# Last pass of a four-layer graph network on Trainium2: ScalarE, not SyncE, issues the reads of the stored target one-hots

## The chip, the cores and the metric

The kernel runs on one core of a Trainium2 chip. The metric is the device time of one launch in microseconds (us); lower is better. The engines of the core run their own instruction streams side by side: TensorE (PE; its weight loads are PEld), VectorE (DVE), ScalarE (ACT), GpSimd (POOL) and SyncE (SP), which here only issues transfers. An engine's sequencer (PEq, ACTq, SPq and so on) handles register steps, semaphore waits and DMA issues. Sixteen DMA engines carry every transfer, whichever engine issued it; SP's transfers stand in queue q1 of the profile, ScalarE's in q10, GpSimd's in q0.

## The reference

A graph of 12,500 nodes with 212,500 edges goes through four pre-norm layers with 32 features; the edges are sorted by target. The change touches only the last layer:

```python
def _L3_gnn_ref(x, src, dst):
    n = x.shape[0]
    msg_sum = jax.ops.segment_sum(x[src], dst, num_segments=n)
    deg = jax.ops.segment_sum(jnp.ones_like(dst, dtype=x.dtype), dst, num_segments=n)
    return msg_sum / jnp.maximum(deg, 1.0)[:, None]
...
h = jnp.maximum(_layernorm(x, axis=-1), 0.0)
x = x + _L3_gnn_ref(h, src, dst)
return x
```

Each node receives the mean of the normalised rows of the nodes that point at it.

## The kernel before

Three of the layers' passes sum rows over edges by matmuls against one-hots, pass `s == 1`, `s == 2` and `s == 4`. The last, `s == 4` (`h == 2` in the code), is the one that changes. Part of the edges, in **blocks** of 32 columns of 128 edges, is sorted by source into 49 buckets of 256 nodes. A block is worked in eight **batches** `q` (`BATCHES`): batch 0 has seven buckets, the others six. For a batch, four engines work one behind another:

- SP spreads the edges' low source numbers over the partitions (`spread_low`, L691, writes `lows`, which the profile calls `idx_a`). It may do so once VectorE has compared the batch four before (`s_from`).
- VectorE compares them with the partition numbers, which gives the source one-hots (`compare_sources`, L1892).
- TensorE picks the source rows with them (`pick`, L1308), and ScalarE copies the picked rows out of PSUM into one of four buffers (`pick_block`, L1004; the profile calls the buffers of `q % 4` = 0, 1, 2, 3 `mem_a`, `mem_b`, `more_rows`, `more_rows`).
- TensorE adds them to the target window with the target one-hots (`send`, L1325) and raises `s_sent`. TensorE's order is pick of batch m+1, send of m, pick of m+2, send of m+1, and so on.

The **target one-hots** of a batch lie in one of four buffers in `O` (`to_oh[4]`, `TO_RING[4]` = 4). They are made in one of two ways. Blocks that the first pass had already seen were stored in `targets_d` then; in the last pass these are read back (`return_targets`, L709). The others are compared again on VectorE (`compare_targets`, L1902). Three blocks make one **turn** (`UNIT[4]` = 3), 24 batches, and there are 13 turns. In blocks e = 0 and e = 1 of a turn the batches 0, 1, 2, 4, 5 and 6 are read back, and batches 3 and 7 are compared (`COMPARED`). In block e = 2 all are compared. That is 156 reads in the pass. The three blocks sum into `ps_t`, `ps_z` and `ps_h`, so these names tell e = 0, 1, 2 in the profile. A read for batch m+2 writes the buffer that the send of m-2 read, so it may be issued once that send is done:

```python
sp.wait_ge(s_sent, ((BEFORE[h] + e) * NBATCH + q + 3 - TO_RING[s]) + i * (UNIT[s] * NBATCH))
```

SP issues at step m first the low numbers of batch m+4, then the one-hots of batch m+2, each behind its own wait and in one queue. Beside this, irregular groups are gathered by GpSimd (L793; ScalarE lays out its row numbers, L907) and summed by TensorE (L1194), four groups a turn.

Of the kernel before, what the change touches and what calls it, by code (L numbers as in the profile page):

```python
# [24 lines left out]
P = 128  # L25
# [22 lines left out]
W2 = 256  # L48
# [4 lines left out]
BATCHES = [(0, 7)] + [(7 + 6 * q, 6) for q in range(7)]  # L53
NBATCH = len(BATCHES)
# [6 lines left out]
TO_RING = {1: 2, 2: 2, 4: 4}  # L61
# [56 lines left out]
def gnn_kernel(nc, x, src, dst, et16, et86, ew, ew1, w0, comp0, w1, b1, w2, comp2, selfw,  # L118
# [14 lines left out]
    with ctx:  # L133
# [357 lines left out]
        def carry_wait(eng):  # L491


            eng.sem_inc(s_carry, 1)
# [63 lines left out]
        def block_of(s, n):  # L558

            turn, e = divmod(n, UNIT[s])  # L560
            return e * TURNS[s] + turn

        def turn_group(s, i, f, k):

            return gathered(s, i, k) + f * (gathered(s, 1, k) - gathered(s, 0, k))
# [25 lines left out]
        def _(sp):  # L591
# [100 lines left out]
                             lows_d[bass.ds(i * (NBK * CAP) + (block_of(s, e) * NBK + b0) * CAP, n * CAP)].partition_broadcast(P)  # L692
                             ).then_inc(s_bc[q % RING], 16)

            def kept_rows(i, n, q):

                b0 = BATCHES[q][0]
                return targets_d[bass.ds(i * P + n * P, P), b0 * W2:(b0 + BATCHES[q][1]) * W2]

            def keep_targets(i, f, q):  # L700

                sp.wait_ge(s_made, (f * NBATCH + q + 1) + i * NBATCH)
# [27 lines left out]
            def spread_and_return(h, ahead, soon, returned):  # L730

                s = (1, 2, 4)[h]
                n = UNIT[s] * NBATCH

                def spread(i, f, m):
                    spread_low(h, i, (f + m // n) * UNIT[s] + m % n // NBATCH, m % NBATCH)

                def give_back(i, f, m):
                    if m % n // NBATCH in returned and (s == 2 or m % NBATCH not in COMPARED):
                        return_targets(h, i, (f + m // n) * UNIT[s] + m % n // NBATCH, m % NBATCH)  # L740

                def turn(i, f, last):
                    for m in range(n):
                        if m + ahead < n or not last:
                            spread(i, f, m + ahead)
                        if m + soon < n or not last:
                            give_back(i, f, m + soon)

                for m in range(ahead):
                    spread(0, 0, m)  # L750
                for m in range(soon):
                    give_back(0, 0, m)
                with sp.Fori(0, TURNS[s] - 1) as i:
                    turn(i, 0, False)
                turn(0, TURNS[s] - 1, True)
# [9 lines left out]
            sp.wait_ge(s_from, BEFORE[2] * NBATCH + RING)  # L765
            edge_array(idx_a, et86, s_et86)
            store_nodes(3, 3, lambda i: cols(H, i, D))
            spread_and_return(2, 4, 2, RETURNED)

            for i in range(NB):  # L770
                sp.wait_ge(blk[4]["u_ready"], i + 1)
# [78 lines left out]
        def _(act):  # L850
# [100 lines left out]
            def pick_and_lay_out(s, h):  # L951
# [43 lines left out]
                            if q % 4 == 2 and (q >= 6 or not first) and q < NBATCH + 4:  # L995
                                next_pair(act, i * TURN + (f + q // NBATCH) * TURN, made, stage_pair)

                def pick_block(i, e):
                    for q, (b0, n) in enumerate(BATCHES):
                        b, at = q % 2, ((BEFORE[h] + e) * NBATCH + q) + i * (UNIT[s] * NBATCH)  # L1000
                        act.wait_ge(s_got, at + 3)
                        act.wait_ge(s_sent, at - 1)
                        carry_wait(act)
                        nc.scalar.copy(slot_rows[q % 4][:, 0:n, :], picked_rows(b)[:, 0:n, 0:SPLIT]).then_inc(s_slot, 1)  # L1004
                        if q in HIDDEN4[e]:
                            lay_out_next(s, i, HIDDEN4[e][q])

                if s == 4:
                    with act.Fori(0, TURNS[s]) as i:
                        for e in range(UNIT[s]):  # L1010
                            pick_block(i, e)
                else:
                    pick_weighed(0, 0, True, False)
                    with act.Fori(0, TURNS[s] - 2) as i:
                        pick_weighed(i, 1, False, False)
                    pick_weighed(0, TURNS[s] - 1, False, True)
# [1462 lines left out]
```

## Time and profile before

| | |
|---|---|
| median of 3 runs | 7553.54 us (7550.62 to 7555.81) |
| the profiled execution | 7557.19 us, its span 7555.4 us |
| last pass, picks to sends | 6901 to 7508 us of the span |
| busy over the whole span | PE 64%, PEld 54%, DVE 59%, ACT 32%, POOL 69% |

Times in the rows are microseconds from the start of the span. A row of the timeline has start, duration, engine, line, operation, output<-input, shapes and count; in brackets stands how long the engine was idle before it and what ended that. In the rows of the chain a DMA piece has its start (the issue), its time to landing, and its tensors. In the rows by stretch (windows) stand the length of the stretch, then for PE, PEld, DVE, ACT and POOL the busy time with the number of instructions, then TensorE's granted clock (1.00 is the full 2.4 GHz), the mean busy share of the 16 DMA engines, and GB/s.

### The profile page before, as it was taken

The numbers are of one execution on the slowest core, as the hardware profiler recorded it, in microseconds if no ns is written. First come the engines' busy times: TensorE is split into PE (matmuls) and PEld (weight loads), VectorE is DVE, ScalarE is ACT, GpSimd is POOL, SyncE is SP. The second block draws the span as 40 slices with busy tenths as digits, with TensorE's granted clock in tenths as the row PEclk, the third lists the DMA queues.
The fourth block names the chain that finished last, engine by engine and source line by source line (L and its number), as shares of the span: only waits on it lengthen the run. The fifth ranks groups of instructions, "written<-read, shape, count | busy, mean of one in ns | idle before, by whom it ended". The sixth has DMA issues, their size and how long they took to land. (4 is left out here: it accounts for less than half of the span.)

```text
span 7555.4 us, 149897 instructions
## 1 busy us (share of the span) xinstructions
PE 4797.7 (64%) x41375; PEld 4089.9 (54%) x41376; DVE 4473.8 (59%) x13819; ACT 2380.2 (32%) x7420; POOL 5213.8 (69%) x5417
## 2 busy tenths in 40 slices
PE   5333333333335677777777776777777777777888
PEld 2222222222224555556666665677777777776777
DVE  5555555557778888885555554444444444446876
ACT  4444444440002222222555555211111111113332
POOL 2777777777765777774766663677777777775774
PEclk6555555555556666666887887555555555557998
DMA  7000000000003444444898988222222222224775
GB/s 175 14 14 14 14 14 14 14 14 13 13 12 98 128 127 126 127 127 118 288 304 293 307 291 271 60 41 41 41 41 41 41 41 41 41 41 123 218 216 167
DMA packets 547178, 778.01 MB, mean 103 GB/s; under 512 B 226905, under 2 KB 383097, under 8 KB 546997
## 3 DMA queue, kind: packets, MB, share of 16 engines
q1 hardware_dynamic: 317381, 416.33, 18.1%
q0 software_dynamic: 173168, 146.14, 11.8%
q10 hardware_dynamic: 56448, 213.62, 7.2%
q8 instruction: 53, 0.87, 0.0%
q14 instruction: 128, 1.05, 0.0%
HBM read 445.42 MB, written 330.21 MB: 103 GB/s over the span
## 5 line engine op out<-in xcount | busy, mean ns | idle before, releaser
L793 POOL DMA_INDIRECT arena<-table,ibuf x3328 | 3151.2, 947 | 1237.4 <-issue 1123.1
L793 POOL DMA_INDIRECT arena<-nodes,ibuf x2080 | 2059.9, 990 | 967.6 <-issue 635.0
L1194 PE MATMUL ps_agg<-mem_a,arena 128*32 128x80 f32 (+1 forms) x3744 | 472.7, 308 | 566.7 <-DVEq L1647 511.8
L1194 PE MATMUL ps_agg<-mem_b,arena 128*32 128x80 f32 (+1 forms) x3744 | 457.4, 301 | 505.7 <-DVEq L1647 492.2
L1194 PEld LDWEIGHTS ps_agg<-mem_a,arena 128*32 128x32 f32 (+1 forms) x3744 | 414.9, 156 | 626.4 <-DVEq L1647 529.7
L1194 PEld LDWEIGHTS ps_agg<-mem_b,arena 128*32 128x32 f32 (+1 forms) x3744 | 400.5, 152 | 555.6 <-DVEq L1647 515.4
L1463 PE MATMUL ps_agg<-tbuf,msg 128*64 128x80 f32 x2496 | 373.6, 344 | 330.7 <-DVE msg L2140 330.7
L1065 ACT ACTIVATE att<-score 128x8 f32<-128x8 f32 x208 | 43.3, 208 | 1649.0 <-DVE score L2131 1649.0
L1463 PEld LDWEIGHTS ps_agg<-tbuf,msg 128*64 128x64 f32 x2496 | 336.0, 226 | 351.8 <-DVE msg L2140 351.8
L916 ACT ACTIVATE tbuf<-O,tbuf 128x49 bf16<-128x49 bf16 x1664 | 448.5, 363 | 76.7 <-DVE H L1814 76.7
L1892 DVE TENSOR_SCALAR tbuf<-idx_a,pcol 128x768 bf16<-128x768 bf16 (+1 forms) x1040 | 402.7, 429 | 93.8 <-issue 44.9
L1666 DVE TENSOR_TENSOR big<-big,ps_agg 32x80 f32 (+1 forms) x468 | 108.4, 232 | 541.9 <-PE ps_agg L1194 476.6
L2123 DVE TENSOR_TENSOR msg<-arena,ps_z 128x256 f32<-128x256 f32 x208 | 87.7, 422 | 551.6 <-DMA arena<-table,ibuf 551.6
L1640 DVE TENSOR_TENSOR arena<-arena,ew_s 128x256 f32<-128x256 f32 x416 | 177.0, 425 | 360.0 <-DMA arena<-table,ibuf 295.7
L1458 PE MATMUL ps_wide<-yw,mem_b 80*128 80x33 f32 x1680 | 380.6, 403 | 1.2 <-ACT yw L1047 1.2
L1458 PE MATMUL ps_h<-yw,mem_b 80*128 80x33 f32 x1664 | 377.0, 403 | 0.0
L1458 PEld LDWEIGHTS ps_wide<-yw,mem_b 80*128 80x128 f32 x1680 | 366.3, 331 | 19.1 <-issue 17.8
L1458 PEld LDWEIGHTS ps_h<-yw,mem_b 80*128 80x128 f32 x1664 | 362.8, 331 | 17.8 <-issue 17.8
L907 ACT COPY ibuf<-idx_a 128x8 int32 x208 | 39.7, 196 | 933.0 <-DMA arena<-table,ibuf 930.9
L1216 PE MATMUL ps_wide<-O,not_before 128*128 128x392 bf16 x156 | 82.3, 528 | 358.3 <-DVE H L1814 358.3
L1450 PE MATMUL ps_wide<-ident,tbuf 128*80 128x128 f32 x1248 | 297.7, 421 | 0.0
L2174 DVE TENSOR_TENSOR big<-big,ps_agg 64x80 f32 x208 | 47.8, 230 | 401.3 <-PE ps_agg L1463 401.3
(417 smaller groups left out, 11941.6 us busy)
## 6 DMA issues: line engine op xcount, KB each, us to landing
table<-tbuf ACTq DMA_DIRECT2D x294, 544.5 KB
idx_a<-lows_d SPq DMA_DIRECT2D x637, 192.0 KB
targets_d<-tbuf SPq DMA_DIRECT2D x182, 384.0 KB, 2.4
H<-targets_d SPq DMA_DIRECT2D x182, 384.0 KB
arena<-table,ibuf POOLq DMA_INDIRECT x3328, 2.4
O<-targets_d SPq DMA_DIRECT2D x130, 384.0 KB
table<-tbuf ACTq DMA_DIRECT2D x98, 495.0 KB
arena<-nodes,ibuf POOLq DMA_INDIRECT x2080
```

The source lines that it names most:

```text
L793: nc.gpsimd.indirect_dma_start(out=INTO[s][:, k, c, 0:WIDTH[s]], out_offset=None, in_=TABLE[s], in_offset=bass.IndirectOffsetOnAxis(ap=ibu ...
L916: op = nc.scalar.mul(moved[:, j, 2 + part, :], by_bucket[:, j, :], of)
L1194: last = nc.tensor.matmul(ps_agg[ROW0[s]:ROW0[s] + CHN[s], 0:WIN], narrow[:, k, c, 0:CHN[s]], onehots[b][:, c, :], start=(c == 0), stop=(c ...
L1216: nc.tensor.matmul(ps_wide[:, r, 0:392], not_before[:, :], bucket_oh[:, at], start=True, stop=False)
L1450: nc.tensor.transpose(ps_wide[0:WIN, c // 4, (c % 4) * P:(c % 4 + 1) * P], rows[:, c, :], ident[:, :])
L1458: last = nc.tensor.matmul(y_own[b][:, c, :], onehot_t[:, c, :], yw[:, :], start=True, stop=True)
L1463: last = nc.tensor.matmul(ps_agg[0:2 * D, 0:WIN], msg[:, c, :], onehots3[k][:, c, :], start=(c == 0), stop=(c == CH - 1))
L1640: V.tensor_tensor(rows, rows, by[:, of].unsqueeze(2).to_broadcast([P, CH, D]), ALU.mult)
L1666: V.tensor_tensor(into, into, ps_agg[r0:r1, 0:WIN], ALU.add)
L1892: op = V.tensor_scalar(from_oh[s][q % 2][:, a, 0:n * CAP], lows[q % RING][:, 0:n * CAP], pcol2[:, a:a + 1], None, ALU.is_equal)
L2123: V.tensor_tensor(msg[:, :, D:2 * D], gbuf[:, k, :, PAIR:PAIR + D], last_in_ps.unsqueeze(2).to_broadcast([P, CH, D]), ALU.mult)
L2174: V.tensor_tensor(into, into, ps_agg[0:2 * D, 0:WIN], ALU.add)
```

## The change

The reads of the stored target one-hots in the last pass leave SP's stream. SP's call becomes `spread_and_return(2, 4, 0, ())`, so it issues the low numbers alone. ScalarE now issues each read (`ask_targets`, called by `ask_ahead`) directly behind its copy of batch m, for batch m+2, with the same wait on `s_sent`. The first two are issued ahead of the loop. The last turn of ScalarE's loop is written out behind it.

```diff
+                def ask_targets(i, e, q):
+
+                    act.wait_ge(s_sent, ((BEFORE[h] + e) * NBATCH + q + 3 - TO_RING[s]) + i * (UNIT[s] * NBATCH))
+                    carry_wait(act)
+                    act.dma_start(to_oh[s][q % TO_RING[s]][:, 0:BATCHES[q][1], :].rearrange("p k w -> p (k w)"),
+                                  kept_rows(i, block_of(s, e), q)).then_inc(s_there[q % TO_RING[s]], 16)
+
+                def ask_ahead(i, m, last):
+                    e, q = divmod(m, NBATCH)
+                    if (e < TURNS[s] * UNIT[s] or not last) and e % UNIT[s] in RETURNED and q not in COMPARED:
+                        ask_targets(i, e, q)
+
...
                         nc.scalar.copy(slot_rows[q % 4][:, 0:n, :], picked_rows(b)[:, 0:n, 0:SPLIT]).then_inc(s_slot, 1)
-                        if q in HIDDEN4[e]:
-                            lay_out_next(s, i, HIDDEN4[e][q])
+                        ask_ahead(i, e * NBATCH + q + 2, last)
+                        if q in HIDDEN4[e % UNIT[s]]:
+                            lay_out_next(s, i, HIDDEN4[e % UNIT[s]][q], e // UNIT[s])
...
-            spread_and_return(2, 4, 2, RETURNED)
+            spread_and_return(2, 4, 0, ())
...
-                    with act.Fori(0, TURNS[s]) as i:
+                    for m in range(2):
+                        ask_ahead(0, m, False)
+                    with act.Fori(0, TURNS[s] - 1) as i:
                         for e in range(UNIT[s]):
-                            pick_block(i, e)
+                            pick_block(i, e, False)
+                    for e in range(UNIT[s]):
+                        pick_block(0, (TURNS[s] - 1) * UNIT[s] + e, True)
```

ScalarE's stream of the last pass, in block e = 0 of a turn, batches 0 to 2, before (the casts are the copies of picked rows, `ibuf` the row numbers for a gather; the names in brackets are the semaphores waited for):

```order
L1004 CAST mem_a<-ps_wide 128x672 [waits slots_rows_summed]
L1001 REGISTER_ALU
L1002 REGISTER_ALU [waits slots_rows_picked]
L1004 CAST mem_b<-ps_wide 128x576 [waits slots_rows_summed]
L1001 REGISTER_ALU
L1002 REGISTER_ALU [waits slots_rows_picked]
L1004 CAST more_rows<-ps_wide 128x576 [waits slots_rows_summed]
L905 ISA
L907 ISA [waits sum1_gathered_0]
L907 COPY ibuf<-src_i 128x8
```

The same place of the same stream in the changed kernel:

```order
L1016 CAST mem_a<-ps_wide 128x672 [waits slots_rows_summed]
L1000 REGISTER_ALU
L1002 ISA [waits slots_rows_summed]
L1002 DMA O<-targets_d 128x1536
L1013 REGISTER_ALU
L1014 REGISTER_ALU [waits slots_rows_picked]
L1016 CAST mem_b<-ps_wide 128x576 [waits slots_rows_summed]
L1013 REGISTER_ALU
L1016 CAST more_rows<-ps_wide 128x576 [waits slots_rows_picked,slots_rows_summed]
L1002 ISA [waits slots_rows_summed]
L1002 DMA O<-targets_d 128x1536
```

A read with its wait now stands between two copies, except behind the copy of batch 1 (batch 3 is compared), and it stands ahead of the row numbers' wait for a gather. SP's stream in the same pass before, where reads and low numbers take turns:

```order
L690 REGISTER_ALU
L691 ISA [waits sources_compared]
L691 DMA idx_a<-lows_d 128x768
L709 ISA [waits slots_rows_summed]
L709 DMA O<-targets_d 128x1536
L690 REGISTER_ALU
L691 ISA [waits sources_compared]
L691 DMA idx_a<-lows_d 128x768
L709 ISA [waits slots_rows_summed]
L709 DMA O<-targets_d 128x1536
```

And SP's stream there in the changed kernel:

```order
L695 REGISTER_ALU
L696 ISA [waits sources_compared]
L696 DMA idx_a<-lows_d 128x768
L695 REGISTER_ALU
L696 ISA [waits sources_compared]
L696 DMA idx_a<-lows_d 128x768
L695 REGISTER_ALU
L696 ISA [waits sources_compared]
L696 DMA idx_a<-lows_d 128x768
```

The reads with their waits are gone from it, and the low numbers follow one another.

## Rows read from the trace of the kernel before

**Rows 1.** Stretches: the last pass; block e = 0 of its fourth turn.

```profile
6901.00:7508.00 607.00, 489.51 (x6555) 428.05 (x6553) 483.02 (x1748) 207.28 (x364) 423.79 (x404) 0.99 0.72 216
7046.00:7061.00 15.00, 12.99 (x183) 11.73 (x181) 11.48 (x35) 6.02 (x11) 11.65 (x12) 1.00 0.95 296
```

**Rows 2.** Chain of work that ended last, in the last pass: shares, and DMA pieces.

```profile
by line: DMA O<-targets_d 25.4%; DVE O L1902 15.8%; DVE tbuf L1892 12.6%; issue 10.5%; PE ps_agg L1194 7.3%; PE ps_wide L1308 4.7%; PE ps_z L1325 4.2%; PE ps_t L1325 3.9%; DMA idx_a<-lows_d 2.3%; PE ps_h L1325 1.4%; SPq L691 1.3%; DVE mem_a
...
7054.85 5.35 DMA O<-targets_d
7066.32 4.48 DMA O<-targets_d
...
7235.87 6.41 DMA O<-targets_d
...
7468.62 7.59 DMA O<-targets_d
```

**Rows 3.** Waits in the last pass: total us, times, longest.

```profile
DVE tbuf L1892 <- DMA idx_a<-lows_d: 16.2, 24, 1.5
PE ps_z L1325 <- DMA O<-targets_d: 14.4, 26, 1.5
...
PE ps_t L1325 <- DMA O<-targets_d: 8.5, 19, 1.8
```

**Rows 4.** Waits of SP's sequencer in the last pass, same columns.

```profile
SPq L691 <- DVE tbuf L1892: 306.0, 251, 3.5
SPq L709 <- PE ps_t L1325: 15.6, 43, 1.6
SPq L709 <- PE ps_z L1325: 8.1, 13, 0.9
```

**Rows 5.** Timeline of ACT: five copies of the fourth turn, one of the eighth.

```profile
7045.00 0.72 ACT L1004 CAST mem_a<-ps_wide 128x672 bf16<-128x672 f32 x1 [1.42 <-PE ps_wide L1308]
...
7052.17 0.64 ACT L1004 CAST mem_a<-ps_wide 128x576 bf16<-128x576 f32 x1 [2.20 <-PE ps_wide L1308]
...
7055.32 0.64 ACT L1004 CAST more_rows<-ps_wide 128x576 bf16<-128x576 f32 x1 [0.53 <-PE ps_wide L1308]
...
7064.95 0.64 ACT L1004 CAST more_rows<-ps_wide 128x576 bf16<-128x576 f32 x1 [1.06 <-PE ps_wide L1308]
...
7066.52 0.64 ACT L1004 CAST mem_a<-ps_wide 128x576 bf16<-128x576 f32 x1 [0.93 <-PE ps_wide L1308]
...
7237.46 0.64 ACT L1004 CAST mem_a<-ps_wide 128x576 bf16<-128x576 f32 x1 [2.24 <-PE ps_wide L1308]
```

**Rows 6.** Timeline of PE: sends, six of them of batches read back.

```profile
7049.34 0.85 PE L1325 MATMUL ps_t<-O,more_rows 128*96 128x256 bf16 x6 [0.20 <-issue]
...
7053.85 0.82 PE L1325 MATMUL ps_t<-O,mem_a 128*96 128x256 bf16 x6
...
7056.50 0.83 PE L1325 MATMUL ps_t<-O,more_rows 128*96 128x256 bf16 x6 [0.15 <-DMA O<-targets_d]
...
7060.34 0.94 PE L1325 MATMUL ps_z<-O,mem_a 128*96 128x256 bf16 x7 [1.02 <-DMA O<-targets_d]
...
7069.31 0.82 PE L1325 MATMUL ps_z<-O,mem_b 128*96 128x256 bf16 x6
...
7070.94 0.83 PE L1325 MATMUL ps_z<-O,more_rows 128*96 128x256 bf16 x6 [0.30 <-DMA O<-targets_d]
...
7242.42 0.83 PE L1325 MATMUL ps_t<-O,more_rows 128*96 128x256 bf16 x6 [0.57 <-DMA O<-targets_d]
```

**Rows 7.** Timeline of ACT: a copy of batch 0, block e = 1.

```profile
7058.06 0.72 ACT L1004 CAST mem_a<-ps_wide 128x672 bf16<-128x672 f32 x1 [0.94 <-PE ps_wide L1308]
```

**Rows 8.** Line L1001 from 7058 to 7059 us: duration ns, first and last start.

```profile
L1001 ACTq ALU_OP  x1: 35/35/35, 7058.2 to 7058.2; - x1
```

**Rows 9.** Line L1124, 4300 to 4320 us: ScalarE's stores of pass 2, columns as above.

```profile
L1124 ACTq DMA_DIRECT2D table<-tbuf x6: 338/343/343, 4303.1 to 4315.6; - x6
```

**Rows 10.** The page's DMA issues: stores of the same one-hots in pass 1.

```profile
targets_d<-tbuf SPq DMA_DIRECT2D x182, 384.0 KB, 2.4
```

More of the change, by code:

```diff
@@ L561, in block_of, with kept_rows @@
             return e * TURNS[s] + turn
+        def kept_rows(i, n, q):
+            b0 = BATCHES[q][0]
+            return targets_d[bass.ds(i * P + n * P, P), b0 * W2:(b0 + BATCHES[q][1]) * W2]
         def turn_group(s, i, f, k):
@@ L693, in spread_low @@
                              ).then_inc(s_bc[q % RING], 16)
-            def kept_rows(i, n, q):
-                b0 = BATCHES[q][0]
-                return targets_d[bass.ds(i * P + n * P, P), b0 * W2:(b0 + BATCHES[q][1]) * W2]
             def keep_targets(i, f, q):
@@ L996, in pick_weighed, with pick_block @@
                                 next_pair(act, i * TURN + (f + q // NBATCH) * TURN, made, stage_pair)
-                def pick_block(i, e):
+                def ask_targets(i, e, q):
[7 more added lines that the diff above has]
+                        ask_targets(i, e, q)
+                def pick_block(i, e, last):
                     for q, (b0, n) in enumerate(BATCHES):
```

## The prediction

> **What bounds the kernel now.** I read first the stretches of the last pass, then its chain of waits, then the waits by engine, and last one turn in order of time. The stretches [rows 1] show a pass of 607 us in which no engine is full: TensorE is busy 490 us, VectorE 483, GpSimd 424, ScalarE 207, at a granted clock of 0.99. Block e = 0 of a turn stands out: there the DMA engines are 95% busy at 296 GB/s. The chain of waits [rows 2] says what ends last. A quarter of it, 25.4% of 607 us or 154 us, is the time from the issue of a one-hot read to its landing; the low numbers' transfers have 2.3%. So in blocks e = 0 and 1 the loop is a ring: send of batch m-2, issue of the read for m+2, landing, send of m+2. Landings on the chain last from 4.48 to 7.59 us here [rows 2]. TensorE itself stood idle for these reads 14.4 + 8.5 = 22.9 us, 45 times [rows 3]. That is all that a faster read can give it directly; VectorE stood 16.2 us, 24 times, for low numbers [rows 3]. In block e = 2 nothing is read back, and VectorE compares every batch.
>
> **When a read is issued.** Before, SP issues the read for m+2 as soon as it has issued the low numbers of m+4 and the send of m-2 is done. 56 of the 156 reads waited for that send, 23.7 us in all [rows 4]; the others only had to come through behind the low numbers, which wait for VectorE (251 waits, 306 us) [rows 4]. How quick SP is when the send was what it waited for: the send at 7053.85 ends 0.82 us later, at 7054.67 [rows 6], and the read is issued at 7054.85 [rows 2], 0.18 us behind.
>
> After, the read for m+2 stands behind ScalarE's copy of batch m, and that copy needs the pick of m, which TensorE begins only after it issued the send of m-2. So the wait on the send never holds ScalarE up, but every read goes out later by about a pick. The question is whether it is later by the copy too. ScalarE's copy of 0.72 us begins at 7058.06 [rows 7], and its sequencer did the next register step at 7058.2 [rows 8], with the copy still running. I take the issue to come 0.25 us behind the start of the copy: SP's 0.18 and one more step for the second wait. If the DMA must wait for the copy's end, it is 0.64 us more [rows 5]. For the read of batch 0 in block e = 1 that gives 7055.32 + 0.25 = 7055.57 against 7054.85 [rows 5, 2]: 0.72 us later.
>
> **What the added DMA costs ScalarE.** Its own stores hold its sequencer 0.34 us each [rows 9]. 156 of them are 53 us over a pass in which it computes 207 of 607 [rows 1]; where copies follow each other quickest their starts lie some 1.2 us apart (0.53 idle and 0.64 busy [rows 5]), and 0.25 + 0.34 = 0.59 us fits behind a start. I cost it at nothing; the cover is ScalarE's idle time. The row numbers for a gather come 0.4 to 0.6 us later four times a turn; GpSimd is busy 424 us of 607 [rows 1] and has that to spare. The first two reads, ahead of the loop, and the written-out last turn cost nothing that I can find; SP's shorter stream saves SP's time only.
>
> **How long a read takes from ScalarE's queue.** No row shows it. The bounds: stores of the same 384 KB landed 2.4 us after the issue [rows 10], though they write where these read; reads from SP took 4.48 us at 7066.32, 5.35 us for the seven buckets at 7054.85, and up to 7.59 us [rows 2]. In its own queue a read no longer stands behind 192 KB of low numbers, which helps; but both draw on DMA engines that are 95% busy [rows 1], and low numbers issued after the read may now pass beside it. I take 4.5 us for 384 KB, at the short end of what SP's reads show, and 5.0 us for the 448 KB of batch 0.
>
> **The sum, on the fourth turn.** A send may start 0.25 + 4.5 + 0.14 = 4.89 us after its copy began, 5.39 us for batch 0. The 0.14 is the step from landing to matmul: 7066.32 + 4.48 = 7070.80, matmul at 7070.94 [rows 2, 6]. "Later" is measured against before, and a delay of one send shifts all copies whose picks come behind it. The rest of the turn's sends have more room than this.
> - Block 0, batch 2: copy 7045.00 + 4.89 = 7049.89, was 7049.34 [rows 5, 6]: 0.55 later.
> - Block 0, batch 6: 7052.17 + 0.55 + 4.89 = 7057.61, was 7056.50: 1.11 later.
> - Block 1, batch 0: its copy's pick came ahead of that send, so 7055.32 + 0.55 + 5.39 = 7061.26, was 7060.34: 0.92 later. The 1.02 us that TensorE had waited there [rows 6] swallows the 1.11.
> - Block 1, batch 5: 7064.95 + 0.92 + 4.89 = 7070.76, was 7069.31: 1.45 later.
> - Block 1, batch 6: 7066.52 + 0.92 + 4.89 = 7072.33, was 7070.94: 1.39 later, where 0.30 of waiting had been.
>
> The turn ends 1.4 us later. Not all turns are like it: in the eighth the read at 7235.87 took 6.41 us and TensorE waited 0.57 us for it; there 7237.46 + 4.89 = 7242.35 against 7242.42 [rows 2, 5, 6], nothing later. I take 1.0 us a turn as the mean of the two sorts, 13 us over 13 turns. Against it stands what low numbers gain from a queue of their own. At most it is VectorE's 16.2 us [rows 3]; with 2.3% of the chain against 25.4% I take 3 us. Sum: +10 us on the profiled execution's 7557.2, so 7567; that execution lay 3.7 us above the median of the runs, so 7564 us as a median, +0.14%.
>
> How this hangs on the landing: 0.1 us more makes the turn 0.3 us longer, since it enters three times (batch 2, then batch 6 or 0, then batch 5), which is 3.9 us over the pass. A landing of 4.2 us gives 7552, 5.0 us gives 7583.
>
> **A rule against the change.** The stretch [rows 1] has the DMA engines at 95% in block 0, so a second queue finds them taken. The Trainium skill, page "DMA: Bandwidth & Descriptors", section "Issuing engines are not separate DMA queues", says that transfers issued by different engines run on the same 16 DMA engines and interleave, and that issuing from several saves only sequencer time. By it the read would land no sooner and the change would only issue later, which is the rival of landings as long as before; no row here shows a read from ScalarE's queue.
>
> **The rivals.** A measurement of this kernel can tell some 0.2%, 15 us, from no change.
> - Forecast, 0.44: landings of 4.2 to 4.8 us; the later issue and the freer queue nearly cancel. 7552 to 7576.
> - Landings of 4.1 us and less, 0.17: standing behind the low numbers was the greater part of the landing. At 3.8 us the sum is 10 - 0.7 x 39 = -17 us: 7537. The floor is 22.9 + 3 us gained, 7528. For it: the low numbers are issued just ahead of each read. Against it: 95% busy.
> - Landings as long as before, 0.20, slower: I put them at 5.0 us, between 4.48 and 5.35 [rows 2], and with the issue 0.7 us later TensorE waits more. 10 + 0.5 x 39 = 29.5 us: 7583. It decides from a landing of about 4.63 us on, where +15 us is reached. For it: 296 GB/s in block 0 [rows 1].
> - ScalarE holds the DMA until its copy has ended, 0.14, slower: 0.64 us in three places of 13 turns is +25 us, 7589. Against it: [rows 8].
> - Anything else, such as the reads delaying a later copy: 0.05.
>
> **How the numbers follow.** The predicted time is the forecast's, 7564 us. Of its 0.44 about 0.31 lie within 15 us of before and 0.13 above. Of the fast landings 0.12 are below 7538.4. The two slower rivals lie nearly wholly above 7568.6. With the rest shared out: faster 0.14, same 0.41, slower 0.45. The range for 8 in 10 runs from 7538, which leaves out about half of the fast landings, to 7592, above both slow rivals' middles.
>
> **What the profile after would show.** Issues of `O<-targets_d` on ScalarE's sequencer, 0.2 to 0.3 us behind the start of a copy if I am right, 0.9 if the copy holds them. Landing pieces on the chain of 4.4 to 4.6 us, with a share still above a quarter. TensorE's wait for these reads, 22.9 us before, at 30 to 45 us. VectorE's 16.2 us of waiting for low numbers mostly gone. The time of the pass, 607 us, at 613 to 620, and nothing moved ahead of it. I am wrong if landings fall below 4 us, if sends wait for copies rather than reads, or if GpSimd's gathers become what is waited for.

## The result, and the profile after

The changed kernel takes 7625.45 us (7618.71 to 7629.61, 4 runs) against 7554.68 us (7550.62 to 7556.03, 4 runs) for the kernel before: a ratio of 1.0092, interval 1.0077 to 1.0107. That is 71 us slower, and 33 us above the top of my range. The profiled execution took 7629.61 us, with a span of 7627.8. From the first copy of the pass to the last it takes 681.8 us instead of 605.1, which is 77 us more. The pass began 6 us sooner in this execution (6895.6 against 6902.1), so nothing was lost ahead of it: the whole loss lies inside.

I went through the same views as before. First the stretches of the changed kernel: the pass, and then three neighbouring pieces of its fourth turn (columns as in [rows 1]).

```profile
6895.00:7580.00 685.00, 516.03 (x6557) 454.25 (x6554) 481.70 (x1749) 209.81 (x364) 434.08 (x403) 0.94 0.66 191
...
7067.00:7072.00 5.00, 5.00 (x78) 4.74 (x74) 4.30 (x14) 2.83 (x5) 3.81 (x4) 1.00 0.91 239
7072.00:7076.00 4.00, 0.51 (x6) 0.50 (x6) 0.55 (x2) 0.64 (x1) 3.08 (x4) 1.00 1.02 362
7076.00:7081.00 5.00, 5.00 (x52) 4.56 (x50) 1.38 (x5) 0.64 (x1) 1.46 (x2) 0.66 0.17 58
```

Two things differ from [rows 1]. The DMA share of the pass has fallen from 0.72 to 0.66, and TensorE's granted clock from 0.99 to 0.94. The pieces show how both come about: TensorE runs full for 5 us, stands for nearly 4 us while the DMA engines are completely taken (1.02, 362 GB/s), and then runs full again but at a granted clock of 0.66 over the 5 us, partly at its lower level of 1.2 GHz, while the DMA engines have next to nothing to do (0.17). Where block e = 0 before had a mean DMA share of 0.95 [rows 1], and between 0.90 and 0.99 in pieces of 3 and 4 us, there are now bursts and gaps.

The waits of the changed kernel in the pass (total us, times, longest), and SP's below them:

```profile
POOL arena L793 <- DVEq L1677: 94.1, 44, 4.5
...
PE ps_z L1342 <- DMA O<-targets_d: 60.7, 26, 3.8
...
DVE tbuf L1909 <- DMA idx_a<-lows_d: 26.3, 22, 3.1
...
PE ps_t L1342 <- DMA O<-targets_d: 21.9, 16, 2.6
```

```profile
SPq L696 <- DVE tbuf L1909: 481.6, 273, 8.1
```

TensorE waits for reads 60.7 + 21.9 = 82.6 us where it was 22.9 [rows 3], and not more often (42 times instead of 45): the waits are longer. They lie nearly all in three places of a turn: block 0 batch 2, block 1 batch 0 and block 1 batch 5, with 1.42, 2.59 and 2.08 us a turn, where it was 0.35, 0.81 and 0.12 us (means of the 13 turns in the trace). VectorE waits 26.3 us for low numbers instead of 16.2 [rows 3]; a queue of their own gave them nothing. SP stands 481.6 us for VectorE's comparison where it stood 306.0 [rows 4], which costs nothing in itself. GpSimd's gathers wait 94.1 us for VectorE, where it was 23.4, but the waits have no line in which an engine waits for a gather.

ScalarE's stream, in order of time, with the issue of a read behind a copy, and two more within 2.6 us:

```profile
7055.45 0.34 ACTq L1002 DMA_DIRECT2D O<-targets_d  x1
...
7068.44 0.64 ACT L1016 CAST more_rows<-ps_wide 128x576 bf16<-128x576 f32 x1 [0.53 <-PE ps_wide L1325]
7068.68 0.34 ACTq L1002 DMA_DIRECT2D O<-targets_d  x1
...
7069.82 0.34 ACTq L1002 DMA_DIRECT2D O<-targets_d  x1
...
7071.23 0.36 ACTq L1002 DMA_DIRECT2D O<-targets_d  x1
```

And SP's low numbers at that time, five issues in 6 us:

```profile
7067.02 6.02 SPq L696 DMA_DIRECT2D idx_a<-lows_d  x5
```

TensorE over the same time. The two waits are for the reads issued at 7055.45 and at 7068.68:

```profile
7061.68 0.85 PE L1342 MATMUL ps_t<-O,more_rows 128*96 128x256 bf16 x6 [2.36 <-DMA O<-targets_d]
7062.46 2.00 PE L1211 MATMUL ps_agg<-mem_a,arena 128*32 128x80 f32 x16
7064.39 1.14 PE L1325 MATMUL ps_wide<-ew_s,tbuf 128*128 128x96 bf16 x12
...
7067.62 0.67 PE L1325 MATMUL ps_wide<-half_tiles,tbuf 128*128 128x96 bf16 x12
...
7075.53 0.94 PE L1342 MATMUL ps_z<-O,mem_a 128*96 128x256 bf16 x7 [3.49 <-DMA O<-targets_d]
7076.40 2.26 PE L1211 MATMUL ps_agg<-mem_b,arena 128*32 128x80 f32 x16
7078.59 1.14 PE L1325 MATMUL ps_wide<-arena,tbuf 128*128 128x96 bf16 x12
```

The same sixteen matmuls of an irregular group took this long in the kernel before, behind the wait of 1.02 us at 7060.34 [rows 6]:

```profile
7061.20 1.29 PE L1194 MATMUL ps_agg<-mem_b,arena 128*32 128x80 f32 x16
```

After the wait of 3.49 us they take 2.26 us instead of 1.29, and the pick behind them 1.14 us for twelve matmuls where 0.67 is usual. A wait like these is paid for a second time. Counted in the trace's clock records, from 5 us behind the first copy to the last, TensorE was at its lower level for 75.1 us, against 3.4 us before. If it had been busy all that time, the same work would have taken 37 us at the full clock, so up to 37 us of the 77 may lie there. Not every long wait has this behind it: of TensorE's 22 waits for reads over 2 us, 14 had a stretch at the lower level that began in them or within 2 us behind them. The others, among them waits of 3.39 and 3.56 us, had none.

The page's queues (packets, MB, share of the 16 engines) and its issues show that the reads moved and that nothing was added. q1 had 416.33 MB before and q10 213.62, so 63 MB went from the one to the other:

```profile
q1 hardware_dynamic: 294917, 353.27, 15.5%
...
q10 hardware_dynamic: 78912, 276.68, 9.7%
...
O<-targets_d ACTq DMA_DIRECT2D x130, 384.0 KB
```

The chain of waits of the changed kernel can't be read over the whole pass, since it has no piece between 6950 and 7450 us. Two landings behind that are these, of 448 and of 384 KB, and both are longer than the 5.0 and 4.5 us that I counted on:

```profile
7540.60 5.48 DMA O<-targets_d
...
7550.85 6.13 DMA O<-targets_d
```

### The profile page after: what moved, and what is told of

It is laid out like the page before. It is cut to its first block and busy times, and to the rows that moved or that the text cites. A ratio compares the mean times of both kernels' runs of the same rounds, so it can differ in the third digit from the quotient of the medians.

```text
span 7627.8 us, 149984 instructions
## 1 busy us (share of the span) xinstructions
PE 4799.7 (63%) x41375; PEld 4096.8 (54%) x41376; DVE 4472.5 (59%) x13819; ACT 2387.3 (31%) x7420; POOL 5229.4 (69%) x5417
```

## The experiments

Two things were changed at once: the queue that a read goes through (**two queues** instead of one), and the moment at which it is issued (**late**, behind pick and copy, instead of **early**, as soon as the send allows). My theory was that both count and that they work on each other; the rivals were that the lateness alone costs the time, that the second queue alone does, and that the clock is only a result of waits and costs nothing itself. Each experiment below was timed beside the kernel before; the table gives medians, the ratio with its interval, and, from the profiled execution, waits in the pass and its length from first to last copy.

| kernel | us | before | ratio | TensorE waits for reads | VectorE for low numbers | first to last copy |
|---|---|---|---|---|---|---|
| before | 7554.68 | | | 22.9 | 16.2 | 605.1 |
| changed | 7625.45 | 7554.68 | 1.0092 (1.0077 to 1.0107) | 82.6 | 26.3 | 681.8 |
| two queues, early | 7571.62 | 7558.07 | 1.0019 (1.0009 to 1.0029) | 31.9 | 35.2 | 624.0 |
| one queue (SP), late | 7579.5 | 7558.07 | 1.0026 (1.0016 to 1.0037) | 42.7 | 21.3 | 620.2 |
| one queue (ScalarE), late | 7591.16 | 7556.43 | 1.0043 (1.0026 to 1.0059) | 46.0 | 26.6 | 636.6 |
| one queue (SP), reads first | 7555.58 | 7558.07 | 0.9998 (0.9988 to 1.0008) | 5.7 | 53.9 | 607.1 |
| changed, with filler matmuls | 7606.21 | 7558.07 | 1.0062 (1.0045 to 1.0079) | 50.4 | 22.4 | 658.9 |
| changed, a quarter of the low numbers' bytes | 7564.08 | 7554.56 | 1.0015 (1.0005 to 1.0025) | 37.8 | 3.7 | 616.1 |

A second table has what the ring of the prediction is made of, at the three places where TensorE's long waits lie (in us, means of 13 turns). The first column is the time from the end of the send that a read waits for to the issue of the read, summed over the three places. The landing is the time from the issue to the last mark of completion in the trace. Some marks are missing there, so the landings are rather too short than too long.

| kernel | send to issue, sum of three | landing, block 0 batch 2 | block 1 batch 0 | block 1 batch 5 | their sum | all 156 reads |
|---|---|---|---|---|---|---|
| before | 1.6 | 4.56 | 5.38 | 4.52 | 14.5 | 5.2 |
| changed | 3.2 | 5.36 | 5.96 | 6.18 | 17.5 | 5.1 |
| two queues, early | 0.7 | 4.67 | 6.09 | 3.98 | 14.7 | 5.1 |
| one queue (SP), late | 2.6 | 4.53 | 4.93 | 5.14 | 14.6 | 4.8 |
| one queue (ScalarE), late | 3.3 | 4.66 | 4.97 | 5.24 | 14.9 | 4.7 |
| one queue (SP), reads first | 0.5 | 3.94 | 5.07 | 3.78 | 12.8 | 4.6 |
| changed, with filler matmuls | 3.4 | 5.34 | 6.11 | 5.92 | 17.4 | 5.1 |
| changed, a quarter of the low numbers' bytes | 3.3 | 4.61 | 4.81 | 4.57 | 14.0 | 4.3 |

The mean of all reads hardly differs between before and changed (5.2 and 5.1 us): some reads with time to spare land sooner (block 0 batch 6 after 3.50 us instead of 5.90), and those that TensorE stands for land later.

**Two queues, early.** ScalarE issues the read ahead of its waits for the pick, so that the send of m-2 holds it, but no longer low numbers ahead of it, as on SP before. Against the changed kernel:

```diff
                     for q in range(NBATCH):
...
+                        ask_ahead(i, e * NBATCH + q + 2, last)
...
                         nc.scalar.copy(slot_rows[q % 4][:, 0:n, :], picked_rows(b)[:, 0:n, 0:SPLIT]).then_inc(s_slot, 1)
-                        ask_ahead(i, e * NBATCH + q + 2, last)
```

> The changed kernel, but ScalarE issues the read for batch m+2 ahead of its wait for the pick of m and its copy, so as early as SyncE did before (send of m-2 done), still from its own queue. Theory A (the lateness of about a pick does it): the pass is back at its old length, 7545 to 7560 us. Theory B (two queues side by side do it: a read of a burst shares the DMA engines with low numbers issued after it, where one queue served it first; and each TensorE wait of over 2 us then halves its clock for some microseconds): the issue comes 0.7 to 1 us earlier, which takes some of the clock drops away, but landings in a burst stay at 6 us and more; 7575 to 7605 us.

It is 14 us slower than before: the second queue alone costs that, although the reads go out a little sooner than on SP (0.7 us against 1.6 over three places). Its waits, in a profiled execution that was the slowest of its ten, 11 us above their median:

```profile
DVE tbuf L1909 <- DMA idx_a<-lows_d: 35.2, 33, 2.9
...
PE ps_z L1342 <- DMA O<-targets_d: 26.6, 23, 3.0
...
PE ps_t L1342 <- DMA O<-targets_d: 5.3, 14, 1.7
```

Neither side gained from being apart. The low numbers are waited for twice as long as before (35.2 against 16.2 [rows 3]), and they took a share of the chain that they had not had:

```profile
by line: DVE O L1919 18.8%; DMA O<-targets_d 17.8%; DVE tbuf L1909 12.1%; issue 10.8%; DMA idx_a<-lows_d 10.2%; PE ps_agg L1211 5.9%; PE ps_wide L1325 5.3%; PE ps_t L1342 4.9%; PE ps_z L1342 3.5%; PE ps_h L1342 1.8%; DVE mem_a L2134 1.6%; D
...
7015.27 7.84 DMA O<-targets_d
...
7058.59 6.25 DMA O<-targets_d
```

The low numbers' 10.2% stand against 2.3% in [rows 2]. My reading is that one queue had served the two streams in the order of their issue, and that with two queues a transfer that is needed next gets only a part of the sixteen engines. The landings at block 1 batch 0 fit that (6.09 us instead of 5.38); at the other two places they are not longer.

**One queue, late.** SP keeps the reads, but waits in the last pass for the pick of batch m instead of for the send of m-2. Against the kernel before:

```diff
-                sp.wait_ge(s_sent, ((BEFORE[h] + e) * NBATCH + q + 3 - TO_RING[s]) + i * (UNIT[s] * NBATCH))
+                if s == 4:
+                    sp.wait_ge(s_got, ((BEFORE[h] + e) * NBATCH + q + 1) + i * (UNIT[s] * NBATCH))
+                else:
+                    sp.wait_ge(s_sent, ((BEFORE[h] + e) * NBATCH + q + 3 - TO_RING[s]) + i * (UNIT[s] * NBATCH))
```

> The kernel before, but SyncE holds the read for batch m+2 until the pick of batch m is done, which is about when ScalarE issues it in the changed kernel (0.15 us earlier); one queue as before. Low numbers behind a held read go out later too. Theory A (lateness): 7600 to 7625 us. Theory B (two queues and the clock): the ring is 0.7 us longer in three places a turn, without the long landings: 7565 to 7585 us.

It is 21 us slower than before. Its waits:

```profile
PE ps_z L1328 <- DMA O<-targets_d: 31.9, 38, 2.4
...
DVE tbuf L1895 <- DMA idx_a<-lows_d: 21.3, 26, 1.7
...
PE ps_t L1328 <- DMA O<-targets_d: 10.8, 19, 1.0
```

So lateness costs 21, the second queue 14, and both together 71. This run is not quite as late as the changed kernel, though: SP issues the read 0.02 us behind the start of the copy, ScalarE 0.23 us (medians), so the send to issue is 2.6 us a turn here and 3.2 there. The next experiment has the full lateness. Neither of the rivals with a single cause holds. TensorE was at its lower clock for 6.8 us here and for 27.3 us in the experiment before, against 75.1 us with both.

**One queue on ScalarE, late.** The low numbers go to ScalarE too, so that one queue carries both again. Against the changed kernel:

```diff
-            spread_and_return(2, 4, 0, ())
...
+                def ask_lows(i, m, last):
+                    e, q = divmod(m, NBATCH)
+                    if e < TURNS[s] * UNIT[s] or not last:
+                        b0, n = BATCHES[q]
+                        act.wait_ge(s_from, ((BEFORE[h] + e) * NBATCH + q + 1) + i * (UNIT[s] * NBATCH))
+                        act.dma_start(lows[q % RING][:, 0:n * CAP],
+                                      lows_d[bass.ds(i * (NBK * CAP) + (block_of(s, e) * NBK + b0) * CAP, n * CAP)].partition_broadcast(P)
+                                      ).then_inc(s_bc[q % RING], 16)
...
+                        ask_lows(i, e * NBATCH + q + 4, last)
...
+                    for m in range(RING):
+                        ask_lows(0, m, False)
```

> Repeat, since in the first try all programs ran some 36% slower. The changed kernel with the low numbers, too, issued by ScalarE, those of batch m+4 ahead of its copy of batch m; the reads stay late, behind the copy. One queue, ScalarE's. Theory B (two queues side by side): 7565 to 7590 us. Rival C (ScalarE's queue or its late issue alone): 7610 to 7630 us or more.

It is 35 us slower than before, with twice as many DMAs issued by ScalarE as in the changed kernel, and yet 36 us less slow than that one. So ScalarE as the issuer isn't what costs 71 us; two queues in place of one is a large part of it.

```profile
PE ps_z L1353 <- DMA O<-targets_d: 33.9, 33, 2.3
...
PE ps_t L1353 <- DMA O<-targets_d: 12.1, 14, 1.7
```

No wait reaches 2.4 us, and TensorE spent 17.1 us at its lower clock. This is the better measure of the lateness alone: 35 us, where the run on SP, with reads issued 0.7 us a turn sooner, has 21. With 14 us for the second queue, 22 us of the 71 are left that neither brings alone (36 us by the run on SP). The second table shows where they lie. Landings at the three places sum to 14.5 us a turn before, to 14.6 and 14.9 with lateness alone, to 14.7 with the second queue alone, and to 17.5 with both. 3.0 us a turn are 39 us over the pass.

**One queue, the read first.** In the kernel before, the two transfers of a step change places: SP issues the read for m+2 ahead of the low numbers for m+4.

```diff
+                        if s == 4 and (m + soon < n or not last):
+                            give_back(i, f, m + soon)
...
-                        if m + soon < n or not last:
+                        if s != 4 and (m + soon < n or not last):
                             give_back(i, f, m + soon)
```

> The kernel before, but at each step of the last pass SyncE issues the read for batch m+2 ahead of the low numbers of m+4, not behind them; one queue. If standing behind 192 KB of low numbers lengthens a read, landings on the chain fall from 4.4 to 5.9 us to about 4 us and the time to 7535 to 7550 us. If the low numbers, held up by a read's wait, become late instead, VectorE's 16.2 us of waiting for them grows: 7555 to 7575 us.

The time doesn't change (0.9998). Its waits:

```profile
DVE tbuf L1894 <- DMA idx_a<-lows_d: 53.9, 53, 2.7
...
PE ps_z L1327 <- DMA O<-targets_d: 3.0, 5, 1.1
...
PE ps_t L1327 <- DMA O<-targets_d: 2.7, 5, 1.0
```

The order in one queue only moves the wait from one stream to the other: 22.9 us for reads became 5.7, 16.2 us for low numbers became 53.9. So in one queue nothing is to be gained by serving the reads first: the low numbers are just as close behind.

**Filler matmuls in the wait.** In the changed kernel TensorE does 18 matmuls whose results nobody reads ahead of the wait for the read of batch 2 of blocks that are the first of a turn, and 34 ahead of batch 0 of the second. These are two of the three places with the long waits; at the third, batch 5 of block 1, 1.74 us a turn are left here.

```diff
+                        for j in range({(0, 2): 18, (1, 0): 34}.get((e % 3, q), 0)):
+                            nc.tensor.matmul(ps_agg[:, 256:256 + SPLIT], ident_h[:, :], ident_h[:, 0:SPLIT], start=True, stop=True)
```

> The changed kernel with matmuls that nobody reads put on TensorE ahead of its wait for the read in two places a turn: 18 (about 1.0 us at full clock) ahead of the send of batch 2, block 0, and 34 (about 1.9 us) ahead of batch 0, block 1. They add 13 x 2.9 = 38 us of TensorE work where it idles now. If the clock that falls to half after the long waits costs a large part of the 70 us, the granted clock of the pass is back near 0.99 and the time falls to 7575 to 7600 us. If the clock is only a by-product, the time stays at 7620 to 7640 us.

TensorE over the same two places of the fourth turn:

```profile
7060.24 0.93 PE L1338 MATMUL ps_agg<-ident_h 128*128 128x96 bf16 x18
7061.44 0.85 PE L1344 MATMUL ps_t<-O,more_rows 128*96 128x256 bf16 x6 [0.27 <-ACT more_rows L1016]
7062.22 1.29 PE L1211 MATMUL ps_agg<-mem_a,arena 128*32 128x80 f32 x16
...
7070.61 1.61 PE L1338 MATMUL ps_agg<-ident_h 128*128 128x96 bf16 x34
7073.69 0.94 PE L1344 MATMUL ps_z<-O,mem_a 128*96 128x256 bf16 x7 [1.47 <-DMA O<-targets_d]
7074.56 1.29 PE L1211 MATMUL ps_agg<-mem_b,arena 128*32 128x80 f32 x16
```

The group of sixteen takes 1.29 us again in both places. The kernel has 13 x (0.93 + 1.61) = 33 us more work for TensorE, and is 19 us faster than the changed one (7606.21 against 7625.45; 23 us when each is set against its own runs of the kernel before). Its waits for reads fell by 32 us, about what the filler fills:

```profile
PE ps_z L1344 <- DMA O<-targets_d: 39.5, 24, 2.8
...
PE ps_t L1344 <- DMA O<-targets_d: 10.9, 13, 1.2
```

TensorE stood or did filler for 50.4 + 33 = 83 us, as long as it stands in the changed kernel without filler (82.6). Nor did reads land much sooner at the three places (17.4 us a turn against 17.5). So the gain isn't from shorter landings, and what else differs is the clock, at the lower level for 13.7 us instead of 75.1. I put its share of the 71 us at about 20 us. What the same filler does to the kernel before could not be measured.

**A quarter of the low numbers' bytes.** In the changed kernel the transfers of low numbers in the last pass, behind the first four, move only the first quarter of each batch. Left out are the other three quarters, where the comparison goes by what the buffer last held; the count of transfers and of all other instructions is the same.

```diff
-                sp.dma_start(lows[q % RING][:, 0:n * CAP],
-                             lows_d[bass.ds(i * (NBK * CAP) + (block_of(s, e) * NBK + b0) * CAP, n * CAP)].partition_broadcast(P)
+                m = n * CAP // (4 if s == 4 and not whole else 1)
+                sp.dma_start(lows[q % RING][:, 0:m],
+                             lows_d[bass.ds(i * (NBK * CAP) + (block_of(s, e) * NBK + b0) * CAP, m)].partition_broadcast(P)
```

> The cut of the low numbers to a quarter in the changed kernel, another try (all programs ran 36% slower in the earlier ones). Theory B (low numbers share the DMA engines with a burst's reads, and that is what makes the read of a burst late): read landings in a burst about 4.5 us, few waits over 2 us, clock of the pass back near 0.99, 7530 to 7570 us. Rival C (late issue or ScalarE's queue in itself): 7590 us and more.

It comes within 9.5 us of the kernel before; 61 of the 71 us are gone.

```profile
PE ps_z L1343 <- DMA O<-targets_d: 28.5, 27, 1.9
...
PE ps_t L1343 <- DMA O<-targets_d: 9.3, 9, 1.2
...
DVE tbuf L1910 <- DMA idx_a<-lows_d: 3.7, 6, 1.2
```

```profile
6915.00:7500.00 585.00, 461.24 (x6212) 404.08 (x6213) 456.47 (x1661) 198.60 (x345) 411.70 (x388) 0.99 0.55 138
```

With less to share, no wait passes 1.9 us and the clock stays at 0.99. The reads go out as late as in the changed kernel (3.3 us a turn), but their landings at the three places are 14.0 us a turn in place of 17.5. So it takes the full traffic of the low numbers to stretch them. The run also has the landings that I had forecast (4.5, 5.0 and 4.5, measured 4.61, 4.81 and 4.57), and took 7564 us, the time of the forecast. That is good for the ring of the prediction, but luck in part: VectorE's waits for low numbers fell by 12.5 us here, where I had counted 3. The same cut might help the kernel before as well, and that control could not be measured. Its waits for both streams sum to 39 us [rows 3]; if it gained all of them, 22 us of the 61 would still be the changed kernel's own. Between 22 and 61 the share stays open, and so does whether it is the order of service or the mere amount of traffic that counts.

**What was not measured.** Twelve further runs, of three controls and of repeats, fell on times in which every program, the kernel before too, took some 36 to 38% longer (10,273 to 10,419 us for the kernel before). No variant differs there by more than 0.22%, not even those that differ above, so they say nothing on the question. They stand here with what was expected of them.

The changed kernel with a quarter of the low numbers' bytes, as above.

> The changed kernel with the low numbers' transfers of the last pass cut to a quarter of their bytes (48 KB in place of 192), after the first four; the rest of the low numbers is left over from earlier batches, so the last layer's sums are left out in this form: the work after the landing is the same. Reads and low numbers still go out from two queues at the same times. Theory B (a read of a burst lands late because the low numbers share the DMA engines with it): the read's landings in a burst fall from 6 to 7 us to about 4.5 us, no TensorE wait is long enough to bring the clock down, and the time lies within 25 us of the same cut made to the kernel before. Rival C (ScalarE's queue is slow in itself, or the ring simply is too long by the late issue): the distance between the two stays at 50 us or more.

Measured: 10281.23 us against 10284.28, ratio 1.0 (0.9983 to 1.0017).

> Repeat of the cut of the low numbers to a quarter in the changed kernel, since the chip ran all programs some 36% slower in the first try. Theory B (low numbers share the DMA engines with a burst's reads): read landings in a burst about 4.5 us, no clock drop from long waits, time within 25 us of the control. Rival C (the late issue or ScalarE's queue in itself): distance to the control 50 us or more.

Measured: 10265.45 us against 10276.86, ratio 1.0001 (0.9978 to 1.0024).

> The cut of the low numbers to a quarter in the changed kernel, third try (all programs ran 36% slower in the first two). By now late reads alone cost some 20 us on SyncE's queue and 35 us on ScalarE's single queue, against 70 us with two queues. Theory B (low numbers share the DMA engines with a burst's reads): read landings in a burst about 4.5 us, no clock drop from long waits, time within 25 us of the control. Rival C: distance to the control 50 us or more.

Measured: 10391.74 us against 10418.74, ratio 0.9986 (0.9965 to 1.0007).

A control: the kernel before with the same cut of the low numbers.

> The control for the one above: the kernel before with the same cut, which leaves out the same part. Both theories: TensorE's 22.9 us of waiting for reads and VectorE's 16.2 us for low numbers fall to a few us; 7525 to 7545 us.

Measured: 10283.45 us against 10284.28, ratio 1.0007 (0.9992 to 1.0022).

> Repeat of the control, the same cut in the kernel before: 7525 to 7545 us by both theories.

Measured: 10250.35 us against 10276.86, ratio 0.9993 (0.9966 to 1.0021).

> The control, the same cut in the kernel before: 7525 to 7545 us by both theories.

Measured: 10428.13 us against 10418.74, ratio 1.0008 (0.9982 to 1.0035).

> The control, another try: the same cut in the kernel before. The changed kernel with the cut took 7564 us. If low numbers in the way of the reads cost the kernel before as well, 7525 to 7545 us, and the late issue alone is worth the 20 to 40 us between the two. If the kernel before is held by something else, 7545 to 7560 us, and with small low numbers the late issue costs next to nothing.

Measured: 10242.41 us against 10272.97, ratio 0.9978 (0.9957 to 0.9999).

> The control, last try: the same cut in the kernel before. The changed kernel with the cut took 7564 us. If low numbers in the way of the reads cost the kernel before as well, 7525 to 7545 us, and the late issue alone is worth the 20 to 40 us between the two. If the kernel before is held by something else, 7545 to 7560 us, and with small low numbers the late issue costs 10 to 20 us.

Measured: 10277.66 us against 10280.28, ratio 0.9997 (0.9974 to 1.002).

One queue on ScalarE, late, as above.

> The changed kernel with the low numbers, too, issued by ScalarE: those of batch m+4 ahead of its copy of batch m, so about as early as SyncE issues them. The reads stay late, behind the copy. All is in one queue again, ScalarE's. Theory B (two queues): like the late reads on SyncE's one queue, 7565 to 7590 us. Rival C (ScalarE's queue or its late issue alone): 7610 to 7630 us, or more, since ScalarE now issues two transfers a batch.

Measured: 10288.55 us against 10284.28, ratio 1.0009 (0.9995 to 1.0023).

A control: one queue on ScalarE, early, both transfers ahead of its waits for the pick.

> The one above, with the reads moved ahead of the copy too: one queue, ScalarE's, and both transfers as early as in the kernel before. If queue number and time of issue are all that matters, 7545 to 7565 us, no difference from before. If issuing from ScalarE costs something in itself (0.34 us of its sequencer for each of two transfers), 7570 us and more.

Measured: 10273.24 us against 10284.28, ratio 0.9993 (0.9973 to 1.0012).

> One queue, ScalarE's, for both transfers, and both as early as in the kernel before. If the number of queues and the time of issue are all that matters: 7545 to 7565 us. If issuing from ScalarE costs something in itself: 7570 us and more, and then 15 us of the distance between the late reads on ScalarE's single queue (7591) and on SyncE's (7579) are explained.

Measured: 10409.88 us against 10418.74, ratio 0.9986 (0.9964 to 1.0008).

A control: the kernel before with the filler matmuls at the same two places.

> Control for the filler: the same matmuls that nobody reads, 2.9 us a turn, in the kernel before, where the waits in these places are 0.2 and 1.0 us and the clock stays up. They should cost 13 x (2.9 - 1.2) = 22 us: 7570 to 7580 us. If they cost less than 10 us, work in these places is free and the filler's gain in the changed kernel is the clock's alone; if the filler gains time here too, it is not the clock that it acts on.

Measured: 10438.45 us against 10418.74, ratio 1.002 (0.9996 to 1.0045).

So it isn't measured how much the filler or the cut would bring to the kernel before.

## Why the prediction was wrong, step by step

**When a read is issued: right.** I gave 0.25 us behind the start of the copy; it is 7068.68 - 7068.44 = 0.24 us (median of the pass 0.23), with the copy of 0.64 us still running. The rival in which ScalarE holds the DMA until its copy has ended is out. ScalarE's 0.34 us for each DMA stayed hidden: TensorE's long waits end with reads, not with copies, and with low numbers on ScalarE as well the kernel was faster than the changed one.

**Which places lengthen: right.** The long waits are at batch 2 of block 0 and batches 0 and 5 of block 1, the three places through which a landing entered my sum. The ring itself holds in size too. Send to issue and landing together are 16.1 us a turn over the three places before, and 1.1 us more with late reads on SP, 2.1 us more with late reads and low numbers on ScalarE, and 4.6 us more in the changed kernel (second table). Times 13 turns that is about 15, 27 and 60 us, where the pass was 15, 32 and 77 us longer. The sends didn't come to wait for copies, and GpSimd's gathers didn't become what is waited for.

**The landing: the term that failed.** I took 4.5 us from issue to landing for 384 KB and 5.0 for 448 KB. The step from issue to matmul, with 0.14 counted in, would have been 4.64 and 5.14. In the fourth turn it was 7061.68 - 7055.45 = 6.23 and 7075.53 - 7068.68 = 6.85 us. Over all 13 turns the landings at the three places were 5.36, 5.96 and 6.18 us (second table), where I had 4.5, 5.0 and 4.5. That is 3.5 us a turn more, and by my own rule 45 us over the pass. I had argued that a read which no longer stands behind low numbers lands sooner. Its first packet does come sooner (384 KB: 1.68 us behind the issue instead of 2.19, medians of 129 reads), but its last doesn't (4.68 instead of 4.57). The rival of landings as long as before was nearer, but no description either: I put it at 5.0 us and 7583 us, and landings stayed as they were only in the mean of all reads. Where TensorE stands for them they grew by 0.6 to 1.7 us. The error below both is that I took one landing for all reads, and took it from reads issued at an even pace. The rule that I set against the change, in the Trainium skill's page "DMA: Bandwidth & Descriptors", section "Issuing engines are not separate DMA queues", held in the direction it gives: issued from two engines, the same transfers landed no sooner on the mean (5.1 against 5.2 us).

**What low numbers gain: wrong in sign.** I counted 3 us gained from a queue of their own. VectorE waits 26.3 us for them instead of 16.2, and 35.2 where the reads are early. In the prediction I wrote that low numbers issued after the read may now pass beside it, and gave that no price.

**What I didn't have at all: the clock, and the bunching.** One is the clock. I priced a wait at its own length. Waits of 2.4 and 3.5 us in the fourth turn are each followed by a stretch at 1.2 GHz, in which the group of sixteen takes 2.0 to 2.3 us instead of 1.29; from the filler I put this at about 20 us. The other is that waits bunch the requests. Behind a long wait several picks and copies follow at once, each asks for a read 1.1 to 1.4 us after the other, and SP adds its own five; so the next reads meet at the DMA engines (1.02) and land late, and then nobody asks (0.17). That landings at the three places are long only with both changes together, and only with the low numbers' full traffic, is measured. That it comes about by this loop of wait and burst is read off the fourth turn and not shown by itself.

The sum with measured values then stands so: 10 us as forecast, 45 us for landings and some 20 us for the clock, which makes 75 for 71 measured. The 3 us that I gave to low numbers as a gain belong on the other side, and how far the terms overlap the runs don't separate; so this is an account of the size and no exact division.

## What to carry to other kernels

Before you give a transfer a queue of its own, ask what it shares the DMA engines with. Here they were 95% busy in block 0, and neither stream gained: reads and low numbers together were waited for 39 us in one queue and 67 us in two. A mean landing hides what matters in a ring of buffers: look up the landing of those reads that an engine stands for, and ask what the next requests do after a wait, since here they came in a burst. When a change lengthens TensorE's waits, read the granted clock behind them too, and price a stretch at the lower level besides the wait itself.

## What the runs showed of the hardware

- Reads of 384 KB had their first packet 2.19 us behind the issue in the kernel before, 1.94 us in a queue of their own with early issue, and 1.91 (SP) and 1.61 us (ScalarE) in one shared queue with late issue; with both changes it was 1.68 us. The last packet came after 4.57, 4.62, 4.50, 4.37 and 4.68 us (medians of 129 reads each). So the sooner first packet is not the second queue's alone, and it says nothing of the last.
- The same read landed after 4.52 us on the mean before and after 6.18 us in the changed kernel (block 1 batch 5), and another after 5.90 and 3.50 us (block 0 batch 6), at a mean of all reads of 5.2 and 5.1 us.
- TensorE, fully busy, had a granted clock of 0.66 over the 5 us behind a wait of 3.49 us, and twelve matmuls took 1.14 us instead of 0.67. The lower level came with 14 of the 22 waits for reads over 2 us in the changed kernel and with 2 of the 14 from 1 to 2 us; in the kernel before, with none of the 6 from 1 to 2 us. 33 us of needless matmuls made the changed kernel 19 us faster.
- ScalarE's sequencer issued a DMA 0.24 us behind the start of a copy of 0.64 us that is ahead of it in the program (median of the pass 0.23).
